# A mask written by ScalarE under half of the shifted scores, and transposes and score products in another order

## What is computed

```python
attn = jnp.einsum('bhqd,bhkd->bhqk', q, k) * scale
block_ids = pos // blk
block_mask = block_ids[:, None] != block_ids[None, :]
causal_mask = pos[:, None] < pos[None, :]
attn = jnp.where((causal_mask | block_mask)[None, None], mask_floor, attn)
attn = softmax(attn, axis=-1)
context = jnp.einsum('bhqk,bhkd->bhqd', attn, v)
```

## Time and profile before

| what | us |
|---|---|
| median of 3 runs (665.19 to 668.53) | 665.48 |
| the profiled execution | 665.03 |
| its span, first to last instruction | 663.2 |
| PE busy | 619.9 (93% of the span) |
| VectorE, ScalarE, GpSimd busy | 404.6, 315.7, 185.2 |
| mean granted clock of TensorE | 0.978 |

### The profile page before, as it was taken

How to read it: one execution, slowest core, us unless ns; L and a number is a source line. 1 busy time by engine, 2 the same in 40 slices (tenths; PEclk the granted TensorE clock), 3 DMA queues, 4 the chain that set the end, 5 groups by cost and what they waited for, 6 DMA issues and landing times.

```text
span 663.2 us, 13983 instructions
## 1 busy us (share of the span) xinstructions
PE 619.9 (93%) x5816; PEld 424.9 (64%) x5816; DVE 404.6 (61%) x623; ACT 315.7 (48%) x478; POOL 185.2 (28%) x264
## 2 busy tenths in 40 slices
PE   5689999999999999999999999999999999869996
PEld 3545667567864667667884657766785566637783
DVE  2786744687467563668557555468647664447554
ACT  3736464356444356257443445437534444417442
POOL 1156640024016561034005662023102763000000
PEclk8599999999999999999999999999999999989999
DMA  8744000034022000025012100004202100000000
GB/s 327 239 111 119 30 3 1 1 83 109 1 60 99 2 2 3 0 48 144 1 27 70 64 3 2 1 14 123 57 0 64 65 2 3 1 1 0 1 1 32
DMA packets 16456, 31.77 MB, mean 48 GB/s; under 512 B 5060, under 2 KB 5828, under 8 KB 16260
## 3 DMA queue, kind: packets, MB, share of 16 engines
q1 hardware_dynamic: 14856, 27.98, 14.5%
q0 software_dynamic: 1152, 2.36, 1.4%
q10 hardware_dynamic: 384, 0.52, 0.3%
HBM read 12.99 MB, written 2.10 MB: 23 GB/s over the span
## 4 chain that ended last, share of the span: by engine, by line
PE 72%; DVE 14%; ACT 9%; issue 4%; DMA 1%; DVEq 0%; SPq 0%; ACTq 0%
PE bank L1622 8%; PE bank L1532 7%; PE bank L1424 5%; PE bank L1428 5%; PE bank L1425 5%; PE bank L1710 4%; PE bank L1560 3%; PE bank L1594 3%; PE bank L1805 3%; PE bank L1807 3%; PE bank L1568 3%; PE bank L1806 3%; PE bank L1831 2%; PE bank L1828 2%; PE bank L1464 2%
## 5 line engine op out<-in xcount | busy, mean ns | idle before, releaser
L1143 DVE TENSOR_REDUCE neg_max<-bank 128x8 f32<-128x1024 f32 x64 | 77.7, 1223 | 46.5 <-PE bank L1560 46.3
L584 POOL TENSOR_SCALAR arena_r<-q_st,const 100x512 fp32r<-100x512 f32 x128 | 87.7, 702 | 47.5 <-ACT q_st L778 47.1
L1332 DVE TENSOR_TENSOR arena<-arena,bank 128x512 f32<-128x512 f32 (+1 forms) x72 | 49.6, 688 | 71.7 <-ACT arena L870 69.9
L1424 PE MATMUL bank<-n_hi,w_lo 128*128 128x512 f32 x184 | 79.8, 434 | 3.3 <-ACT n_hi L733 1.7
L870 ACT ACTIVATE arena<-bank 128x512 f32<-128x512 f32 (+1 forms) x72 | 43.0, 598 | 82.0 <-PE bank L1807 47.0
L1532 PE MATMUL bank<-mask 128*128 128x512 bf16 x256 | 77.9, 386 | 3.6 <-ACT n_hi L683 2.2
L1428 PE MATMUL bank<-n_lo,w_hi 128*128 128x512 f32 x184 | 74.4, 404 | 0.2
L1425 PE MATMUL bank<-n_hi,w_hi 128*128 128x512 f32 x184 | 74.1, 403 | 0.0
L807 ACT ACTIVATE tile_f<-bank 128x1024 f32<-128x1024 f32 x56 | 57.2, 1024 | 33.4 <-PE bank L1594 33.2
L565 POOL TENSOR_TENSOR k_wide<-n_lo,head_of 128x512 fp32r<-128x512 f32 x30 | 32.6, 1089 | 103.9 <-DMA n_lo<-k_st 103.9
L539 POOL TENSOR_TENSOR tile_f<-tile_f,const 128x512 f32<-128x512 f32 x16 | 22.3, 1394 | 121.5 <-ACT tile_f L719 121.5
(11 more groups left out here) (180 smaller groups left out, 1167.9 us busy)
## 6 DMA issues: line engine op xcount, KB each, us to landing
q_st<-arena_r SPq DMA_DIRECT2D x96, 64.0 KB, 2.0
k_st<-arena_r SPq DMA_DIRECT2D x52, 64.0 KB, 2.0
k_st<-arena_r POOLq DMA_DIRECT2D x36, 64.0 KB, 2.4
h_next<-in_x SPq DMA_DIRECT2D x4, 512.0 KB, 3.6
tile_f<-in_x SPq DMA_DIRECT2D x4, 512.0 KB, 4.4
out<-arena SPq DMA_DIRECT2D x4, 512.0 KB, 2.8
n_lo<-k_st SPq DMA_DIRECT2D x24, 64.0 KB, 2.0
n_hi<-q_st SPq DMA_DIRECT2D x24, 64.0 KB, 2.0
```

The lines of the kernel that those rows point to most:

```text
L584: last = nc.gpsimd.tensor_scalar(q_ex[u % 2][0:KS, :, hh, :], src, con("head")[0:KS, hh:hh + 1], 1.0, ALU.mult, ALU.mult)
L1143: nc.vector.tensor_reduce(neg_max[:, 2 * a:2 * a + 2, MROW:KS], slot(("s1", n)).rearrange("p a (h s) -> p a h s", s=P), AX_X, ALU.max, neg ...
L1332: nc.vector.tensor_tensor(pair_tmp[n % 2][0:width], silu_out[n % 2][0:width], up, ALU.mult)\
L1424: nc.tensor.matmul(to, wl[:, at], n_hi[:, kt, :], start=kt == 0, stop=False)
```

## The change

ScalarE copies the mask, broadcast over 8 heads, into the two banks of s2 of half a = 0 of each unit u > 0 (`preset`, a copy of 128 x 1024 to PSUM), in program order behind the exponentials of the unit before; PE then does these two products without the two mask products, and waits for `mask_set`. For this, s2 of a = 0 has banks 0 and 1 to itself, both s1 of a unit share banks 2 and 3, and t and s2 of a = 1 share banks 4 and 5. On PE, the transposes of unit u + 1 now follow the first s2 of unit u (before: the transposes of unit u + 2 at the end of unit u), and the contexts of 2u stand between s2 of 2u + 1 and the second s1. On ScalarE, `max_to_rows` of unit u + 1 is the first step of unit u (before: that of unit u + 2 behind the exponentials).

```diff
--- before.py
+++ after.py
@@ -331,6 +331,7 @@
         lora_hi = signal("lora_hi", 4)
         powers_set = signal("powers_set", 1)
         exp_half = signal("exp_half", 2)
+        mask_set = signal("mask_set", UNITS - 1)
         lora_lo = signal("lora_lo", 4)
         gu_ready = signal("gu_ready", FT * VARIANTS)
         ff_silu = signal("ff_silu", FT * VARIANTS)
@@ -349,12 +350,14 @@
         fills = [("s1", 0), ("s1", 1), ("t", 0), ("s1", 2), ("s1", 3), ("t", 1)]
         slot_of = dict(zip(fills, (0, 1, 0, 1, 0, 1)))
         for u in range(UNITS):
-            for a in range(2):
-                fills += [("s2", 2 * u + a)] + ([("s1", 2 * (u + AHEAD) + a)] if u + AHEAD < UNITS else [])
-            if u + AHEAD < UNITS:
-                fills += [("t", u + AHEAD)]
-        for n, what in enumerate(fills[6:]):
-            slot_of[what] = (n + 2) % 3
+            further = u + AHEAD < UNITS
+            fills += [("s2", 2 * u)]
+            fills += [("t", u + 1)] if 1 <= u < UNITS - 1 else []
+            fills += [("s1", 2 * (u + AHEAD))] if further else []
+            fills += [("s2", 2 * u + 1)]
+            fills += [("s1", 2 * (u + AHEAD) + 1)] if further else []
+        for kind, n in fills[6:]:
+            slot_of[kind, n] = 2 if kind == "s2" and n % 2 == 0 else 0 if kind == "s1" else 1
         freed_by = {"s1": max_done, "t": max_rows, "s2": exp_done}
 
         def slot(fill):
@@ -778,6 +781,12 @@
                 nc.scalar.copy(q_st[MROW:KS, half * GQ:(half + 1) * GQ, blk * P:(blk + 1) * P], src)\
                     .then_inc(max_rows.sem, 1)
 
+            def preset(row, u):
+
+                act.wait_ge(exp_done.sem, exp_done.count(row, 2 * u - 1))
+                to = slot(("s2", 2 * u)).rearrange("p g (h s) -> p (g h) s", s=P)
+                nc.scalar.copy(to, mask[:, 2:3, :].broadcast_to([P, 2 * GH, P])).then_inc(mask_set.sem, 1)
+
             def tails_stacked():
 
                 act.wait_ge(chunk_hi[5].sem, 1)
@@ -790,6 +799,8 @@
             def row_steps(row, last):
 
                 for u in range(UNITS):
+                    if 1 <= u < UNITS - 1:
+                        max_to_rows(row, u + 1, 0)
                     for a in range(2):
                         n = 2 * u + a
                         act.wait_ge(s2_ready.sem, s2_ready.count(row, n + 1))
@@ -807,13 +818,13 @@
                             nc.scalar.activation(prob[a], scores, ACT.Exp, scale=SCALE).then_inc(exp_done.sem, 1)
                         if row == n == 0:
                             max_to_rows(0, 1, 0)
+                    if u + 1 < UNITS:
+                        preset(row, u + 1)
                     if u == 0:
 
                         act.wait_ge(out_ready.sem, out_ready.count(row, 0))
                         act.wait_ge(front.shifted.sem, front.shifted.count(row, 1))
                         nc.scalar.copy(h[:], h_next[:]).then_inc(h_moved.sem, 1)
-                    if u + AHEAD < UNITS:
-                        max_to_rows(row, u + AHEAD, 0)
                     if row == 0:
 
                         if u == 0:
@@ -1586,13 +1597,20 @@
                             half_stacked(pe, row, half, 0)
                         if u == BLOCKS:
                             pe.wait_ge(ones_back.sem, 16)
-                    to = fill(row, "s2", n, 0)
-                    for g in range(2):
-                        masked(to[:, g, :], 2)
+                    written = u > 0 and a == 0
+                    if written:
+
+                        pe.wait_ge(mask_set.sem, mask_set.count(row, u))
+                        to = slot(("s2", n))
+                    else:
+                        to = fill(row, "s2", n, 0)
+                        for g in range(2):
+                            masked(to[:, g, :], 2)
                     for g in range(2):
                         gq = 2 * a + g
                         last = nc.tensor.matmul(to[:, g, :], k_st[0:KS, half * GQ + gq, blk * P:(blk + 1) * P],
-                                                q_ex[u % 2][0:KS, gq], start=False, stop=True)
+                                                q_ex[u % 2][0:KS, gq], start=False, stop=True,
+                                                skip_group_check=written)
                     last.then_inc(s2_ready.sem, 1)
 
                 def contexts(n):
@@ -1628,15 +1646,18 @@
                     shifted_scores(0)
                 max_transposed(row, 1, 0)
                 for u in range(UNITS):
-                    for a in range(2):
-                        if row or u or a:
-                            shifted_scores(2 * u + a)
-                        if u + AHEAD < UNITS:
-                            scores_for_max(row, 2 * (u + AHEAD) + a, 0)
-                    for a in range(2):
-                        contexts(2 * u + a)
-                    if u + AHEAD < UNITS:
-                        max_transposed(row, u + AHEAD, 0)
+                    further = u + AHEAD < UNITS
+                    if row or u:
+                        shifted_scores(2 * u)
+                    if 1 <= u < UNITS - 1:
+                        max_transposed(row, u + 1, 0)
+                    if further:
+                        scores_for_max(row, 2 * (u + AHEAD), 0)
+                    shifted_scores(2 * u + 1)
+                    contexts(2 * u)
+                    if further:
+                        scores_for_max(row, 2 * (u + AHEAD) + 1, 0)
+                    contexts(2 * u + 1)
                     if not is_last:
 
                         if u == 2:
```

## The result

The changed kernel takes 670.55 us (median of 6 runs, 668.96 to 673.76), the kernel before on the same chip 665.49 (6 runs, 665.19 to 668.53): a ratio of 1.0073, with an interval of 1.0047 to 1.0099. It is slower by 5.1 us. The forecast was 669.9.

The account below looks back on a forecast made before the run. PE was taken to bound plain units, ScalarE's order three other places. Row changes of 2 x 2.1 + 1.0 - 0.3 = +4.9 us on the profiled 665.03 gave 669.9, range 665.5 to 674.

Parts of the forecast that it names:

- Part 1: Plain unit, first s2 to transposes: 0.56 us; a pair of mask products saves 0.455, less 0.10 of weight load.
- The middle between a hidden and an exposed load: Weight load of products directly behind the contexts: 0 if hidden, 0.19 us if exposed, taken as 0.10.
- Part 2: Contexts cut in two halves on PE: 0.23 us more in each of units 0 to 5.
- The waits in a plain unit: Other engines' results in a plain unit come before PE needs them; the mask copy has 0.85 us to spare.
- Part 3: Unit 4 of rows 0 to 2: PE's second s2 waits behind front_squares; unit takes 7.4 us, loss 1.0 a row.
- Part 4: Units 6 and 7 of rows 0 to 2, bound by ScalarE: +1.35 us a row; row 3's tail 8.9, +0.1.
- Row 0's weight splitting: Units 1 to 5 of row 0: splitting moves into ScalarE's free time, so row 0 loses 1.12 us less.
- The sum: Attention rows: +2.1 us each for rows 1 and 2, +1.0 row 0, -0.3 row 3, total +4.9.
- the clock: Rival: TensorE's clock falls in the tails of three rows, +7.5 us, 677.4 in all; chance 0.04.

Follow-up runs that it names:

- experiment 2: The changed kernel without ScalarE's mask copies, so PE writes all masks itself: 675.61 us, ratio 1.0149.
- experiment 3: The changed kernel with both halves of the contexts together again at the unit's end, behind the second s1: 673.42 us, ratio 1.0111.
- experiment 4: The changed kernel with each copy of the mask made twice, one behind the other: 679.66 us, ratio 1.0207.
- sister kernel: The changed kernel with only the second front_squares moved, from behind unit 6 to behind unit 7's exponentials: 668.8 us, ratio 1.0034.
- experiment 5: front_squares moved later: in the changed kernel first 666.15 us, second 668.8, both 661.72; in the kernel before, both 665.82.

## Why the prediction was right

It said 669.9 and slower; 670.55 came. Its steps, one by one:

- **Part 1, the mask products.** Predicted 0.56 from the first s2 to the transposes, measured 0.57; a pair gives 0.34 (experiment 2). The middle between a hidden and an exposed load came out right, but by luck, not as a half-hidden load: the load of keys starts with its product, and the mask load that stands in its place in experiment 2 does so too and is shorter. The Trainium skill ("TensorE: Matmul & The Clock Gate", Step-by-step: what each phase is for) says that PE pulls a weight load ahead of products in flight where the row groups don't conflict or the load goes to the background buffer. For this pair, keys' weights behind 32-column products, the trace shows the loader idle for 0.20 us and nothing pulled ahead; whether either condition held, no run shows.
- **Part 2, the halves.** Predicted +0.23, measured +0.25 (experiment 3, by subtraction); the rows of the changed kernel give 0.24 (two halves of 1.01 for 1.88, and 1.01 from the second s2's masks to the contexts for 0.91). The plain unit came at 5.97 for 6.00: the sum kept 0.48 for the transposes, which now stand behind products of keys and take 0.44 (213.71 to 214.15). So of the 0.34 of the mask products a plain unit keeps 0.15, with the 0.04 of the transposes in it.
- **The waits in a plain unit.** The copy of the mask takes 1.02, as taken from the exponential. Its spare time was given as 0.85; experiment 4 puts it at 0.8. None of the waits appeared in plain units.
- The Trainium skill ("ScalarE: Activation LUTs", Step-by-step: what each stage is for) says that ScalarE writes faster to PSUM than to SBUF. Here the copy of 128 x 1024 to PSUM took 1.02, no less than the exponential of the same size to SBUF; the two differ in more than where they write to.
- **Part 3, unit 4.** Predicted a wait of 1.37 and a unit of 7.4; measured 1.33 and 7.39 (first products at 232.76 to 240.15). The chain behind it ran as forecast too: from the transposes of unit 3 to the second s2 of unit 4 it is 8.77 (227.36 to 236.13), where the prediction's marks give 9.38 - 0.56 = 8.82. Moving the first squares gave it back, 4.4 us in all by the medians: that is the cause, shown.
- **Part 4, the tails.** Predicted 11.2, measured 11.18 in row 1. That ScalarE's queue sets it is shown by the mask copied twice (+1.04) and by the second shifts and squares moved (-1.4). Row 3: 8.88 (557.18 to 566.06) for 8.9. Row 0's weight splitting: its units 1 to 5 now take 34.55 (56.71 to 91.26) against 34.56 in row 1 (213.71 to 248.27), so the 1.12 of before are gone to the last tenth.
- **The sum.** Predicted +2.1 for rows 1 and 2 each, +1.0 for row 0, -0.3 for row 3, together +4.9; measured +1.93, +1.91, +1.06 and -0.47, together +4.4. The plain units' 0.03, 17 times, is about that difference. That the median came within 0.7 of the forecast all the same is in part luck: the changed kernel's runs spread over 4.8 us, and the profiled execution lost time between the attentions and behind the last, for which the prediction had no term.

Of the rivals, the clock was the one that I had put in the wrong place. I looked for it in the tails, and gave it 0.04. It does not appear in the attentions of the profiled execution of the changed kernel; but in a sister kernel with the same wait it fell in unit 4 twice. The changed kernel's runs spread over 4.8 us; whether such falls are part of that can't be seen from one profiled execution.

What the prediction didn't ask is whether the loss was part of the change or of its surroundings. It was of the surroundings: six instructions of another layer norm in ScalarE's queue in each row, two of which made ScalarE wait for VectorE (2.52 us in unit 3). The two stalls cost 4.4 us (experiment 5) and some 4.2 us (three tails of 1.4 in the traces), together twice the 4.0 us that the change brings where they are taken out.

## What to carry to other kernels

When work goes from a full engine to one that has time on average, list what is queued on that other engine at each place, and what that waits for: an instruction that was harmless behind a buffer of slack becomes the bound when something in front of PE's next product moves behind it. Look for those instructions first; moving them can be cheaper than giving up the change, and here it turned 0.7% slower into 0.6% faster. And cost a reordering by the groups it cuts: what is saved in one group can be paid at the seams of others (here 0.34 saved, 0.24 paid).

## What the runs showed of the hardware

- Cutting a unit's 32-column products in two, with full products between the halves, cost PE 0.24 to 0.25 us a unit.
- Behind 32-column products the next weight load did not start early: the loader sat idle for 0.20 us ahead of a 0.19 us load of keys, a shorter mask load, and the transposes' load in the kernel before. The same was seen behind full products (0.27 us, 214.83 in the kernel before), so it is not shown to be a matter of the 32 columns.
- The granted clock fell to half behind a wait of 1.33 us amid otherwise full work (0.50 from 234.43 to 237.85), which cost 1.5 us; it did so in two of three rows of one execution, in one of three behind a wait of 2.5 us, and in none of the three rows of the changed kernel's profiled execution.
